# Masking the context once, the null key and value as a further row, and the last folded values through more banks

## What is computed

```python
kv = context @ Wkv
k, v = jnp.split(kv, 2, axis=-1)
nk = jnp.broadcast_to(null_kv[0], (b, HEADS, 1, DIM_HEAD))
nv = jnp.broadcast_to(null_kv[1], (b, HEADS, 1, DIM_HEAD))
k = jnp.concatenate([nk, k], axis=2)
v = jnp.concatenate([nv, v], axis=2)
sim = jnp.einsum('bhid,bhjd->bhij', q, k)
sim = jnp.where(full_mask[:, None, None, :], sim, max_neg)
attn = jax.nn.softmax(sim.astype(jnp.float32), axis=-1).astype(sim.dtype)
out = jnp.einsum('bhij,bhjd->bhid', attn, v)
```

## Time and profile before

| | |
|---|---|
| Median of 3 runs | 1119.86 us (1117.01 to 1123.49) |
| Profiled execution | 1123.39 us, span 1121.7 us |
| TensorE clock granted, mean | 0.96 |
| PE busy | 1050.5 us (94%) |
| DVE busy | 940.9 us (84%) |
| ACT busy | 696.8 us (62%) |
| POOL busy | 480.2 us (43%) |
| Transfers | 83.31 MB |

### The profile page before, as it was taken

The page is one execution under the profiler, slowest core; times in us unless marked ns, Lnnn a source line. Parts: engine busy times, 40 slices in busy tenths (PEclk is TensorE's granted clock), DMA queues, the critical chain, the costliest instruction groups (busy, mean ns, idle before and its releaser), DMA issues.

```text
span 1121.7 us, 21070 instructions
## 1 busy us (share of the span) xinstructions
PE 1050.5 (94%) x6538; PEld 893.8 (80%) x6538; DVE 940.9 (84%) x2544; ACT 696.8 (62%) x1839; POOL 480.2 (43%) x543
## 2 busy tenths in 40 slices
PE   8999999998799888887798999999999899999997
PEld 6877788887688666443698999999999878788876
DVE  6799998886677699899566799999998788888885
ACT  2576777774355789578776677777776523333333
POOL 2335445442000477676001256666665443433343
PEclk9999999998699999689699999999999999999999
DMA  9000000000224387699301410111100000000000
GB/s 280 16 2 1 1 1 1 1 2 1 87 113 180 138 271 269 207 351 354 114 1 53 123 50 2 48 48 48 48 2 1 1 1 29 19 19 19 19 19 29
DMA packets 50647, 83.31 MB, mean 74 GB/s; under 512 B 4715, under 2 KB 36287, under 8 KB 50559
## 3 DMA queue, kind: packets, MB, share of 16 engines
q1 hardware_dynamic: 49183, 81.43, 21.3%
q10 hardware_dynamic: 1376, 0.79, 0.4%
HBM read 45.98 MB, written 36.23 MB: 73 GB/s over the span
## 4 chain that ended last, share of the span: by engine, by line
PE 42%; DVE 6%; issue 1%; POOL 1%; ACT 1%; DMA 1%; DVEq 0%; POOLq 0%; ACTq 0%
PE m_ps L2482 12%; PE a_ps L1282 10%; PE a_ps L1352 9%; PE f_ps L2383 5%; PE a_ps L1301 3%; PE m_ps L2506 1%; DMA k_raw<-vw_scratch 1%; PE a_ps L1331 1%; PE m_ps L2530 1%; DVE m_xl L2691 1%; DVE a_sm L1484 0%; DVE a_PTl L1508 0%; DVE a_mx L1500 0%; PE m_ps L2518 0%; DVE m_g L2678 0%
## 5 line engine op out<-in xcount | busy, mean ns | idle before, releaser
L1373 ACT ACTIVATE a_U<-a_ps,a_mx 128x80 f32<-128x80 f32 x512 | 125.7, 331 | 27.2 <-DVE a_mx L1500 24.4
L1443 POOL TENSOR_TENSOR a_xrs<-a_xve,mhalf 128x1 f32<-128x1 f32 x32 | 31.0, 969 | 156.6 <-DVE a_xve L1572 156.6
L2598 POOL TENSOR_TENSOR m_half<-m_half 128x512 f32<-128x512 f32 x32 | 41.0, 1281 | 118.1 <-ACT m_half L2558 118.1
L1450 POOL TENSOR_TENSOR a_U<-a_U,a_rc 128x1280 f32<-128x1280 f32 x32 | 74.6, 2333 | 35.9 <-DVE a_rc L1490 35.9
L2565 ACT ACTIVATE m_ex<-m_ls 128x8 f32<-128x8 f32 x32 | 6.7, 209 | 131.0 <-DVE m_ls L2654 131.0
L2482 PE MATMUL m_ps<-m_wh,m_xh 128*128 128x512 f32 x256 | 86.1, 417 | 0.0
L2230 POOL TENSOR_SCALAR f_sg<-f_sg 128x1024 f32<-128x1024 f32 x24 | 37.4, 1559 | 104.2 <-ACT f_sg L2119 103.8
L969 PEld LDWEIGHTS a_ps<-vals,a_PT 128*128 128x128 f32 x640 | 79.5, 198 | 2.2 <-issue 0.4
L2482 PE MATMUL m_ps<-m_wh,m_xl 128*128 128x512 f32 x256 | 80.5, 395 | 0.0
L2482 PE MATMUL m_ps<-m_wl,m_xh 128*128 128x512 f32 x256 | 80.2, 394 | 0.0
L1083 DVE TENSOR_SCALAR a_U<-a_ps 128x320 f32<-128x320 f32 x128 | 59.3, 484 | 24.6 <-PE a_ps L876 15.7
(11 more groups left out here) (270 smaller groups left out, 3343.4 us busy)
## 6 DMA issues: line engine op xcount, KB each, us to landing
up_scratch<-f_ub SPq DMA_DIRECT2D x24, 512.0 KB, 3.0
f_ul<-up_scratch SPq DMA_DIRECT2D x24, 512.0 KB, 5.7
key_scratch<-p_keys SPq DMA_DIRECT2D x8, 640.0 KB, 6.8
vw_scratch<-p_vw SPq DMA_DIRECT2D x16, 320.0 KB, 5.8
k_raw<-key_scratch SPq DMA_DIRECT2D x8, 640.0 KB, 5.3
k_raw<-vw_scratch SPq DMA_DIRECT2D x4, 1280.0 KB, 6.0
h_scratch<-f_hh SPq DMA_DIRECT2D x8, 512.0 KB, 2.7
h_scratch<-f_hl SPq DMA_DIRECT2D x8, 512.0 KB, 3.2
```

The costliest lines, as they stand in the source:

```text
L1373: last = act.activation(U[a.p][:, h * KP:(h + 1) * KP], bank(a, g)[:, (h % 4) * KP:(h % 4 + 1) * KP], ACT.Exp, bias=mx[a.p][:, h:h + 1])
L1450: pool.tensor_tensor(heads(U[a.p]), heads(U[a.p]), rc[a.p][:].unsqueeze(2).broadcast_to([P, H, KP]), ALU.mult).then_inc(s_N, 1)
```

## The change

Five parts, by the names above.

- Context masked once. `masks` now has the product of `ctxT` with the mask in its second part (96 x 640), so a masked key's column of the context is zero. The context is stored after that, at the end of attention 0. `nm` is now two single rows, one that marks masked places and one that is 1 at the null key's place; SP stores two rows of 320 instead of two tiles of 128 x 320.
- The null row. The context in the fold stage gets a 97th partition: the masked-place row in its first half, the null-place row in its second. The key weights get the null key as 97th row of their first half (four copies of 64 for two buffers), the value weights the null value in their second. `load_small` issues 12 transfers instead of 6, and the first two `load_values` two more each. The products contract 97 rows in that half. `mask_key` becomes a copy, `keep_key`, on DVE; `mask_value` becomes `keep_value`, a copy on ACT; `null_key` and `null_value` are gone.
- The last pair. `folded_value(7, 0)` goes into `KB` and `VB`, which are free by then; `folded_value(7, 1)` waits only for the copies of pair 6, and is staged in a key buffer instead of its value buffer. `rows_max(4)` uses another bank and waits for the last `key_out`.
- Exponential first. ACT runs an exponential on one column of `nneg` ahead of attention 1's loop; its result isn't used.
- `value_high(0)` and `value_low(0)` come one step later in attention 1.

The diff, cut to its core:

```diff
-        if part == 1:
-            dve.tensor_scalar(nm[:], mb[:], -1.0, 1.0, ALU.mult, ALU.add).then_inc(s_nv, 1)
-            dve.tensor_reduce(nneg[:], mb[:, :, 0:NKEY], AX.X, ALU.add).then_inc(s_nv, 1)
-            dve.wait_ge(s_nv, 4)
-            dve.tensor_scalar(nm[:], nm[:], self.nk[:, 0:1], None, ALU.mult).then_inc(s_nv, 1)
-            dve.tensor_scalar(nneg[:], nneg[:], float(-NKEY), None, ALU.add).then_inc(s_nv, 1)
+        if part == 0:
+            dve.wait_ge(self.s_mk, 16)
+            dve.memset(mb[:], 0.0).then_inc(s_nv, 1)
+            dve.wait_ge(s_nv, 1)
+            dve.tensor_copy(mb[:, :, 0:NKEY], self.m8[:, :, 0:NKEY]).then_inc(s_nv, 1)
+            dve.wait_ge(s_nv, 2)
             return
-        dve.wait_ge(self.s_mk, 48)
-        dve.memset(mb[:], 0.0).then_inc(s_nv, 1)
-        dve.wait_ge(s_nv, 1)
-        dve.tensor_copy(mb[:, :, 0:NKEY], self.m8[:, :, 0:NKEY]).then_inc(s_nv, 1)
-        dve.wait_ge(s_nv, 2)
+        ctxT = self.ctxT[:].rearrange("p c b k -> p c (b k)")
+        dve.tensor_scalar(nm[:], mb[:], -1.0, 1.0, ALU.mult, ALU.add).then_inc(s_nv, 1)
+        dve.tensor_reduce(nneg[:], mb[:, :, 0:NKEY], AX.X, ALU.add).then_inc(s_nv, 1)
+        dve.tensor_tensor(ctxT, ctxT, mb[0:CP].rearrange("p b k -> p (b k)").unsqueeze(1).broadcast_to([CP, CK, B * KP]),
+                          ALU.mult).then_inc(s_nv, 1)
+        dve.wait_ge(s_nv, 4)
+        dve.memset(nm[32:64], 0.0).then_inc(s_nv, 1)
+        dve.tensor_scalar(nneg[:], nneg[:], float(-NKEY), None, ALU.add).then_inc(s_nv, 1)
+        dve.wait_ge(s_nv, 6)
+        dve.memset(nm[32:64, :, NKEY:NKEY + 1], 1.0).then_inc(s_nv, 1)
...
+    def store_context(self, sp):
+        sp.wait_ge(self.s_nv, 5)
+        sp.dma_start(self.cscr, self.ctxT[:].rearrange("p c b k -> p (c b k)")).then_inc(self.s_cs, 16)
 
     def store_masks(self, sp):
-        sp.wait_ge(self.s_nv, 6)
-        for i, m in enumerate((self.mb, self.nm)):
-            sp.dma_start(self.mscr[i], m[:].rearrange("p b k -> p (b k)")).then_inc(self.s_ms, 16)
-
-    def store_context(self, sp):
-        sp.wait_ge(self.s_cTe, 4)
-        sp.dma_start(self.cscr, self.ctxT[:].rearrange("p c b k -> p (c b k)")).then_inc(self.s_cs, 16)
+        sp.wait_ge(self.s_nv, 8)
+        for i in range(2):
+            sp.dma_start(self.mscr[i:i + 1], self.nm[32 * i:32 * i + 1].rearrange("p b k -> p (b k)")
+                         ).then_inc(self.s_ms, 16)
...
-        sp.dma_start(self.ctxT[:].rearrange("p c b k -> p (c b k)"), self.cscr).then_inc(self.s_small, 16)
-        for i, m in enumerate((self.mb, self.nm)):
-            sp.dma_start(m[:], self.mscr[i]).then_inc(self.s_small, 16)
-        for half in (slice(0, D1), slice(D1, P)):
-            sp.dma_start(self.nv[half, 0:1], w["L1_xattn_null_kv"][1].rearrange("(d a) -> d a", a=1)
+        sp.dma_start(self.ctxT[0:CP].rearrange("p c b k -> p (c b k)"), self.cscr).then_inc(self.s_small, 16)
+        for k in range(CK):
+            sp.dma_start(self.ctxT[CP:CP + 1, k, :, :].rearrange("p b k -> p (b k)"), self.mscr[k:k + 1]
                          ).then_inc(self.s_small, 16)
+        for i in range(2):
+            for r in range(4):
+                sp.dma_start(self.wk[i][CP:CP + 1, 0, r * D1:(r + 1) * D1], w["L1_xattn_null_kv"][0:1, :]
+                             ).then_inc(self.s_small, 16)
...
+        if m < 2:
+            for r in range(2):
+                sp.dma_start(self.wv[m][CP:CP + 1, 1, r * D1:(r + 1) * D1], self.w["L1_xattn_null_kv"][1:2, :]
+                             ).then_inc(self.s_wv[m], 16)
...
-            last = pe.matmul(self.KB[:, 0:B * KP], self.wk[m // 2 % 2][:, k, m % 2 * P:(m % 2 + 1) * P],
-                             self.ctxT[:, k, :, :],
+            rows = CP + 1 if k == 0 else CP
+            last = pe.matmul(self.KB[:, 0:B * KP], self.wk[m // 2 % 2][0:rows, k, m % 2 * P:(m % 2 + 1) * P],
+                             self.ctxT[0:rows, k, :, :],
                              start=(k == 0), stop=(k == CK - 1))
         last.then_inc(self.s_k, 1)
...
+    def ends_early(self, m, half):
+
+        return m == self.NM - 1 and half == 0
+
+    def value_banks(self, m, half):
+
+        return (self.KB, self.VB) if self.ends_early(m, half) else self.WB
+
+    def staging(self, m, half):
+
+        if m == self.NM - 1 and half == 1:
+            return self.keys[0][0:KP].rearrange("p k b n -> p (k b n)")[:, 0:4 * D].rearrange("p (h n) -> p h n", h=2)
+        return self.stage[half][:]
+
     def folded_value(self, pe, m, half):
         if half == 0:
             pe.wait_ge(self.s_ve, m + 1)
             pe.wait_ge(self.s_wo[m % 2], 16 * (m // 2 + 1))
-        if 2 * m + half >= 1:
+        if self.ends_early(m, half):
+            pe.wait_ge(self.s_ke, self.NM)
+        elif m == self.NM - 1:
+            pe.wait_ge(self.s_We, 4 * m)
+        elif 2 * m + half >= 1:
             pe.wait_ge(self.s_We, 2 * (2 * m + half))
         for b in (2 * half, 2 * half + 1):
             for hh in range(2):
-                last = pe.matmul(self.WB[hh][0:KP, (b % 2) * D:(b % 2 + 1) * D],
+                last = pe.matmul(self.value_banks(m, half)[hh][0:KP, (b % 2) * D:(b % 2 + 1) * D],
                                  self.VT[m % 2][hh * D1:(hh + 1) * D1, b * KP:(b + 1) * KP],
                                  self.wo[m % 2][hh * D1:(hh + 1) * D1, :], start=True, stop=True)
         last.then_inc(self.s_W, 1)
...
         act.wait_ge(self.s_W, 2 * m + half + 1)
-        if m >= 1:
+        if m == self.NM - 1 and half == 1:
+            act.wait_ge(self.s_ks[0], 16 * self.NM // 2)
+        elif m >= 1:
             act.wait_ge(self.s_st[half], 16 * m)
         for hh in range(2):
-            act.copy(self.stage[half][:, hh, :], self.WB[hh][0:KP, :]).then_inc(self.s_We, 1)
-
-    def mask_key(self, dve, m):
-        if m == 0:
-            dve.wait_ge(self.s_small, 6 * 16)
+            act.copy(self.staging(m, half)[:, hh, :], self.value_banks(m, half)[hh][0:KP, :]).then_inc(self.s_We, 1)
+
+    def keep_key(self, dve, m):
         dve.wait_ge(self.s_k, m + 1)
         if m >= 2:
             dve.wait_ge(self.s_A, 4 * (m - 1))
-        dve.tensor_tensor(self.k1[m % 2][:], self.KB[:, 0:B * KP], self.mb[:],
-                          ALU.mult).then_inc(self.s_km, 1)
-
-    def mask_value(self, dve, m):
-        dve.wait_ge(self.s_v, m + 1)
+        dve.tensor_copy(self.k1[m % 2][:], self.KB[:, 0:B * KP]).then_inc(self.s_ke, 1)
+
+    def keep_value(self, act, m):
+        act.wait_ge(self.s_v, m + 1)
         if m >= 2:
-            dve.wait_ge(self.s_W, 2 * (m - 1))
-        dve.tensor_tensor(self.VT[m % 2][:], self.VB[:, 0:B * KP], self.mb[:],
-                          ALU.mult).then_inc(self.s_vm, 1)
-
-    def null_key(self, pool, m):
-        pool.wait_ge(self.s_km, m + 1)
-        pool.tensor_tensor(self.k1[m % 2][:], self.k1[m % 2][:], self.nm[:], ALU.add).then_inc(self.s_ke, 1)
-
-    def null_value(self, pool, m):
-        pool.wait_ge(self.s_vm, m + 1)
-        pool.tensor_copy(self.VT[m % 2][:].rearrange("p (b k) -> p b k", b=B)[:, :, NKEY],
-                         self.nv[:, 0:1].broadcast_to([P, B])).then_inc(self.s_ve, 1)
+            act.wait_ge(self.s_W, 2 * (m - 1))
+        act.copy(self.VT[m % 2][:], self.VB[:, 0:B * KP]).then_inc(self.s_ve, 1)
...
+            act.activation(mx[1][:, 0:1], c["nneg"][:, 0:1], ACT.Exp)
             for t in range(FIRST, LAST + 1):
                 body(At(t))
-                if t == FIRST + 1:
+                if t == FIRST + 2:
                     for q in range(4):
                         value_high(0, q)
...
-                if t in (FIRST + 2, FIRST + 3):
+                if t in (FIRST + 3, FIRST + 4):
                     for q in range(2):
-                        value_low(0, 2 * (t - FIRST - 2) + q)
+                        value_low(0, 2 * (t - FIRST - 3) + q)
...
-        top = [ps[6], ps[7], ps[6], None, ps[0]]
+        top = [ps[6], ps[7], ps[6], None, ps[2]]
...
                 p1.folded_value(pe, NM - 1, 0)
                 p1.folded_value(pe, NM - 1, 1)
+                pe.wait_ge(p1.s_Ae, 4 * NM)
                 rows_max(pe, 4)
...
                 p1.key_out(act, 0, 1)
+                p1.keep_value(act, 0)
...
                     p1.value_out(act, m - 1, 0)
                     if m < NM:
+                        p1.keep_value(act, m)
                         p1.key_out(act, m, 2)
...
-                p1.null_key(pool, 0)
                 pool.wait_ge(s_sc, SCALED)
                 for u in range(4):
                     rounded(u)
-                    if u == 0:
-                        p1.null_key(pool, 1)
-                        p1.null_value(pool, 0)
                 for m in range(1, NM + 1):
                     rounded(3 * m + 1)
-                    if m < NM:
-                        p1.null_value(pool, m)
                     rounded(3 * m + 2)
-                    if m + 1 < NM:
```

(8 more changed lines are left out.)

41 lines of the change are left out of this document (18 added, 23 removed).

## The result

The changed kernel takes 1115.95 us in the median of 20 runs (1106.68 to 1120.33), the kernel before 1120.87 (1117.01 to 1126.19); the ratio is 0.9943, with a 95% interval of 0.9925 to 0.9960. That is 6.4 us faster by the ratio, 4.9 by the medians; 7.2 was forecast. A second comparison of the same two kernels gave 0.9934 (0.9908 to 0.9961), 7.4 us. (The ratios are of fast runs alone; one execution of twice_the_issues, 1463.86 us at a granted clock of 0.645, is left out.)

The account below looks back on a forecast made before the run. PE was the largest part of the chain of waits (42%), with full DMA transfers holding the fold stage. 0 + 0.6 − 3.0 − 4.8 = −7.2 us, from the 1119.86 median to 1112.7 us; range 1107.5 to 1118.5.

Parts of the forecast that it names:

- D: Start of attention 1, from ACT's first quantised down-weight piece to last residual row: table load and tile copy ahead, −4.8 us.
- B: Up stage: twelve small-load issues make the store behind them, for which ACT waits, land later; +0.6 us.
- A, end of attention 0: Masks' second part grows by up to 1.5 us, covered by DVE's 1.89 us idle for PE; cost 0.
- the rival noted for merged_small: Noted for that run: how DVE's and POOL's operations fall over each other sets the up stage, 94.4 to 95.5 us.
- C, fold stage proper: Fold stage before its tail: DMA queue holds it, so work taken off DVE and POOL becomes waiting; 0 us.
- queue with room: Rival, fold stage: the queue isn't the limit, DVE sets the pace; −5.9 us there, 1109.8 in all; chance 0.20.
- ACT's pace: Rival, fold stage: ACT sets the pace and its copies cost 3.4 us; +0.4 there, 1116.1 in all; chance 0.22.
- C, tail: End of fold stage: last folded values use other banks, rows_max runs at about 536.6; −3.0 us.
- The change doesn't do what it says: Rival: table loaded again behind value_high, or tail banks still wait; about −4 us, 1116; chance 0.03.
- The slower rival: Up stage: twelve small-load issues at 1.58 us each stall ACT's store; +7.7 us in all, 1127.6; chance 0.05.

Follow-up runs that it names:

- twice_the_issues: The changed kernel with each of the ten rows in load_small loaded in two halves, 22 issues instead of 12, same bytes; ratio 0.9939 to the kernel before.
- after_again: The changed kernel itself, run and profiled once more; ratio 0.9934 to the kernel before.
- d_alone: The kernel before with only the new start of attention 1: exponential ahead of the loop, value_high(0) and value_low(0) a step later; ratio 0.9952.
- merged_small: The changed kernel with 4 small loads instead of 12: mask rows loaded as the context's 97th row, the null key's four copies in one transfer per buffer; ratio 0.9990.
- tail_alone: The kernel before with only the last pair's folded values through the other banks and rows_max in its new bank; ratio 0.9984.
- without_d: The changed kernel with the start of attention 1 as before; ratio 0.9978 to the kernel before.
- keep_on_dve: The changed kernel with the value product copied out by DVE instead of ACT; ratio 0.9939 to the kernel before.

## Why the prediction was right, step by step

It was right in sign and size: −7.2 forecast, −6.4 and −7.4 measured, 1115.95 in the range. The time itself is 3.3 us over the 1112.7; 1.0 of that is the kernel before, whose median rose from 1119.86 to 1120.87 with more runs. That the sum came out so close is in part luck: D was 0.6 less than forecast, and B rests on a reason that failed. Of its steps:

- **A, end of attention 0: 0.** Its cover was read in a stretch of low clock (0.50 from 284 to 287 us). The masks' part took 1.0 us more than before (273.26 to 275.45, for 1.19 us before). DVE in the changed kernel:

```profile
273.88 0.81 DVE L371 TENSOR_TENSOR ctxT<-ctxT,mb 96x640 f32<-96x640 f32 x1
...
275.48 0.42 DVE L1120 TENSOR_TENSOR xs<-a_ps,xs 128x256 f32<-128x256 f32 x1
```

There is no idle time left in front of the residual row, where the earlier trace rows had 1.89. PE's last products took 1.13 us here and ended at 274.44, where they had taken 2.07 in the profile before; the granted clock is 1.00 here (272 to 275.5 us). So in an execution at full clock up to 1.0 us of the masks shows; in after_again DVE still waited 0.91 for PE and nothing did.
- **B, small loads: +0.6.** The reason failed. Twelve issues took 4.30 us, 0.36 each, not 6.0 to 6.8, and the store behind them landed in 4.2 us instead of 5.3. So ACT went on 32.7 us after the second maximum, where it had been 33.5 before: 0.8 sooner, not 0.6 later (32.4 to 33.1 in all eight profiles with the twelve issues, 33.1 to 33.5 in the three with six). The up stage was longer all the same, 94.4 to 95.7 in the nine kernels with ten or more rows loaded singly (95.1 in the mean), 93.6 to 94.9 in the three with the mask tiles (94.4). So sign and size came out right by luck. (The upper end is 401.9 + 5.3 − 403.75 = +3.4 by its own terms, not +3.3.) The step that failed is that each microsecond of ACT's wait lengthens the stage ("nothing behind it has slack"). The trace shows who sets its length. It is DVE: from 26 us behind the second maximum to the third it is idle 2.2 us of 67.6 before and 1.4 of 69.4 after, of which the wait for PE's spread of the last maxima at the very end takes 1.5 and 1.4. Its 48 reductions take 1.21 us each in both. Its 24 products of gate and up (L2265 before, L2276 after) don't; the windows of this one line over the stage, with DVE's busy time, PEclk, DMA share and GB/s, before and after:

```profile
370.45:464.09 93.64, 30.10 (x24) 0.93 0.69 242
```

```profile
360.00:455.37 95.37, 32.88 (x24) 0.93 0.66 231
```

That is 2.8 us more of DVE's work in a stage that grew by 1.7. In the four profiles in which ACT went on at 33.4 us or later (before, d_alone, twice_the_issues, merged_small) the 24 take 30.1 to 30.2 us; in the ten in which it went on sooner 31.0 to 32.9, also in tail_alone, which has the old masks. POOL is at work during 1.1 us of a product in the mean in the changed kernel, 0.7 before. So a store that lands sooner goes with longer products on DVE, as the rival noted for merged_small has it; that POOL's nearness is the cause is argued, no run changes it alone.
- **C, fold stage proper: 0.** Held. DVE's maximum was ready 72.49 us after the third `gmax` before and 73.8 in d_alone; 72.24 in the changed kernel, 71.6 in after_again; 71.6 in tail_alone, which has the old masks, and 73.7 in without_d, which has the new ones. POOL's work became waiting, as said. The rival "queue with room", −5.9, fell: taking work from DVE and POOL didn't shorten the stage, and taking bytes away seems to have. "ACT's pace" fell with keep_on_dve, although the sign named for it, DVE waiting over 4.4 us for ACT, did show (7.1): the sign was a bad one, since d_alone, where ACT has no copy more, has 6.1. The 3.4 us of the eight copies was right by luck: the earlier trace rows give 16.2 / 32 = 0.51 us for a copy of `key_out` with what overlaps, not 0.42, so 4.1 in all; 430 ns each was measured. The picture of a queue that only bytes fill is too simple, though: 1.38 MB less gave 2.5 us, not 4.0.
- **C, tail: −3.0.** Measured 2.9, and 2.9 is what the forecast's own terms give, since `rows_max` can't start before DVE's maximum at 536.76. As said, this maximum is next.
- **D: −4.8.** Measured −4.2 in the changed kernel and −4.2 in d_alone, both against before, and −3.9 for the changed kernel against without_d. The mechanism was right, table and tile ahead, PE at the full clock. Oversized was the last gate: the products wait for the exponentials until 601.84, 71.8 us after D's start, for which 613.3 − 541.9 = 71.4 was forecast. Behind it 0.5 us is lost where 0.4 was kept back for `value_low`, and it is lost there: DVE has the last residual row behind `value_low`, and PE waits for this row 1.08 us, where it had been 0.67 before.

```profile
612.30 1.55 DVE L565 TENSOR_TENSOR VW_low<-k_raw,VW_high 128x640 fp32r<-128x640 f32 x2
...
614.78 1.06 PE L1316 MATMUL a_ps<-ident,a_U 128*128 128x128 f32 x8 [1.08 <-DVE xs L2351]
```

- **"The change doesn't do what it says"** is out by the order of the rows. **The slower rival**, a stall at the small loads, didn't happen here, yet merged_small shows its mechanism whole: a store held for 10.8 us, and nearly all of the change's gain gone (0.9990).

## What to carry to other kernels

Cut two traces at the same events and compare the stages before subtracting their spans; here one stage, of which the change touches only the last microseconds, differed by 11 us. Ask of every stage which engine has no idle time in it before pricing a wait of another: the wait of B was on an engine that didn't set the pace. Where a queue is full over a whole stage, work taken off the other engines turned into waiting, and what can be had is at the stage's edges: the two places that paid were a chain of copies through too few banks behind the last unit, and a queue in which something that waits for a load stood ahead of something small that others waited for. And when a cover is idle time in front of a slow engine, look at the clock of that stretch: at full clock the cover may be gone.
